# Causal attention in half chunks of 64 tokens, router steps on GpSimd, six sort steps moved behind the attention

## The chip, the cores and the metric

The kernel runs on one core of one Trainium2 chip. The metric is the device time of one execution in microseconds (us). Engines are named as in the profile: PE is TensorE (PEld its weight loads), DVE is VectorE, ACT is ScalarE, POOL is GpSimd, SP is SyncE.

## What is computed

Two transformer blocks on 4 sequences of 1024 tokens with 128 features. The part that changes is the attention of the first block, a causal linear attention with 16 heads of 8 features, each lifted to 64 positive features:

```
q_prime = relu(einsum('bhld,hdm->bhlm', q, proj))
k_prime = relu(einsum('bhld,hdm->bhlm', k, proj))
kv_cumsum = cumsum(einsum('bhlm,bhld->bhlmd', k_prime, v), axis=2)
context = einsum('bhlm,bhlmd->bhld', q_prime, kv_cumsum)
norm = einsum('bhlm,bhlm->bhl', q_prime, cumsum(k_prime, axis=2))
out = context / (norm[..., None] + 1e-06)
```

Behind it stands a mixture of 64 experts, whose router sorts the scores of all tokens for each expert (`order = argsort(-router_scores, axis=0)`, groups of 64 sorted scores, the best groups kept), and then the second block.

## The kernel before

`causal_attention` walks over 32 chunks of P = 128 tokens, 8 chunks to a sequence (`NC`), 4 chunks to a token tile of 512 (`s = t // 4`, phase `ph = t % 4`). Each engine has its program written out by hand, chunk by chunk, and they meet at semaphores. Nothing is scheduled by a tool: an engine does its instructions in the order of its own `chunk(t)`.

What PE does in one chunk: a mask into the bank of the odd heads (L732), the scores of 8 of the 16 heads (`scores(t, 0)`, L739), the chunk's contribution to the running state (`state`, L750), the features of the next chunk (`features`, L705), a transposition of the last chunk's output (`by_token`, L779), the output that comes from the state of the chunks before (`from_state`, L760), the mask and the scores of the other 8 heads (`scores(t, 1)`), `back` (L784), the output that comes from the chunk's own scores in two parts (`from_chunk`, L770), and the keys of the next chunk by token (`keys_by_token`, L716). DVE takes the scores of the even heads out of their bank with the causal mask (L991, twice a chunk), ACT those of the odd heads (L916, twice). DVE adds up the state (L999, L1002) and divides (`divide`, L1009 to L1013). ACT takes out the features (L902) and the keys (L910).

All f32 matmuls are two instructions in the trace. Scores use tiles of the array of 64 rows by 128 columns (even heads in the upper, odd heads in the lower half of the rows), `state` tiles of 128 by 64, `from_state` and `from_chunk` tiles of 128 by 32, `features` and `keys_by_token` of 32 by 128.

Spread over the four phases of a token tile is other work: the projections of the next tile (`project`, L55 to L57, phase 2), `out_proj` (L788), and the router of the last tile: the residual sum (`add_x`, L1020), the layer norm (`centre` L492, `square`, `take_centred` L543, `variance` L497, `normalise` L549 and L551, `h_high`, `h_low` L558), the logits, their softmax and `scores_back`. From chunk 12 on DVE also has steps of the sort in its queue, in four pieces of each chunk (`sort(t, part)`; one step is L449 and L450). `HELD = 25` is the number of steps of the third sort that are done there; the other 20 are done in the next stage, between DVE's router steps for the last tile, before the fourth sort with the experts' `products`.

## Time and profile before

| | us |
|---|---|
| median of 3 runs | 1006.01 |
| lowest, highest | 1004.88, 1008.31 |
| span of the profiled execution | 1005.2 |
| attention, first mask to the end of chunk 31 | 52.3 to 378.7 |
| its tail to the next stage's first instruction | 378.7 to 388.8 |
| mean granted clock of PE over the span | 0.943 |

The span runs from the first to the last instruction and lies 0.8 us under the median; nothing else of the profiled execution's time is known. In the rows, a time is counted from the start of the span. PE works its instructions off in overlap, so the distance from start to start tells what a group costs, not its duration. The granted clock is 1.00 at 2.4 GHz and 0.50 at 1.2 GHz.

### The profile page before, as it was taken

Reading aid. Unit: us, or ns where it says so; the run is one execution under the profiler, and the core shown is the slowest. Engines: PE = TensorE matmul, PEld = TensorE weight load, DVE = VectorE, ACT = ScalarE, POOL = GpSimd, SP = SyncE. Lnnn points to the kernel's source line nnn. Section 1 sums busy time; section 2 is a strip of 40 time slices with the busy share of each in tenths; the row PEclk is TensorE's granted clock in tenths of the full one; section 3 lists DMA queues with packets and bytes.
Section 4 is the critical chain, followed back from the end, with each engine's and each line's share of the span. In section 5 each row is a group of like instructions: output and inputs, shape, how many; then the busy total and the mean of one; then the engine's idle time right before and its main releaser. Section 6 shows DMA issues by size and latency. Waiting matters only on the chain. (4 is left out here: it accounts for less than half of the span.)

```text
span 1005.2 us, 19673 instructions
## 1 busy us (share of the span) xinstructions
PE 862.9 (86%) x7294; PEld 478.1 (48%) x7294; DVE 741.8 (74%) x1404; ACT 456.6 (45%) x810; POOL 181.9 (18%) x150
## 2 busy tenths in 40 slices
PE   7498999999989885799997988999998787699885
PEld 4266666666656551233443432444433555345543
DVE  3535546787878886999978777888887446689985
ACT  4545656566545551566676862111111255423232
POOL 4250000000000001000004584333332000033340
PEclk9779999999989996899998989999999798899998
DMA  4060000000000000366784768787873000000001
GB/s 129 21 146 2 3 3 2 2 3 2 2 3 2 3 1 1 149 259 241 273 303 168 280 237 321 256 280 270 288 262 137 1 1 1 0 11 11 22 11 31
DMA packets 49671, 103.96 MB, mean 103 GB/s; under 512 B 9968, under 2 KB 24112, under 8 KB 49456
## 3 DMA queue, kind: packets, MB, share of 16 engines
q1 hardware_dynamic: 45360, 100.68, 28.4%
q10 hardware_dynamic: 4224, 2.10, 0.8%
q8 instruction: 57, 0.93, 0.4%
q14 instruction: 30, 0.25, 0.1%
HBM read 53.48 MB, written 48.23 MB: 101 GB/s over the span
## 5 line engine op out<-in xcount | busy, mean ns | idle before, releaser
L1231 PE MATMUL bank<-RS,Wd 128*128 128x512 f32 x256 | 131.5, 603 | 8.8 <-DVE RS L1294 8.6
L1294 DVE TENSOR_TENSOR RS<-so_ug,bank 128x512 f32<-128x512 f32 x128 | 84.1, 672 | 24.0 <-PE bank L1217 13.2
L902 ACT ACTIVATE att_qk<-bank 128x512 f32<-128x512 f32 x128 | 66.8, 602 | 45.0 <-PE bank L705 44.6
L1196 POOL TENSOR_TENSOR so_ug<-so_ug 128x512 f32<-128x512 f32 x48 | 62.3, 1298 | 108.6 <-DMA so_ug<-hidden 108.6
L739 PE MATMUL bank<-att_qk 64*128 64x128 f32 x1024 | 77.2, 292 | 0.0
L1231 PEld LDWEIGHTS bank<-RS,Wd 128*128 128x128 f32 x256 | 47.3, 192 | 59.3 <-issue 28.8
L739 PEld LDWEIGHTS bank<-att_qk 64*128 64x128 f32 x1024 | 64.7, 194 | 20.1 <-issue 20.1
L991 DVE TENSOR_TENSOR att_am<-bank,causal 128x512 f32<-128x512 f32 x64 | 44.0, 687 | 40.9 <-PE bank L739 40.9
L1537 POOL TENSOR_TENSOR so_made<-so_ug 128x512 f32<-128x512 f32 x23 | 35.6, 1564 | 155.7 <-DVE bank L1730 144.6
L1560 ACT ACTIVATE so_ug<-bank,bu 128x512 f32<-128x512 f32 x80 | 54.7, 684 | 17.2 <-PE bank L57 17.1
L1510 POOL MEMSET so_below<- 128x128 f16 x1 | 0.2, 205 | 313.1 <-POOLq L142 313.1
L55 PE MATMUL bank<-Hhi,Wgh 128*128 128x512 f16 x128 | 49.7, 388 | 4.9 <-DVE so_made L1688 4.7
L916 ACT ACTIVATE att_am<-bank 128x512 f32<-128x512 f32 x64 | 38.5, 601 | 27.1 <-PE bank L739 26.6
L910 ACT ACTIVATE att_kt<-bank 128x512 f32<-128x512 f32 x64 | 34.7, 594 | 35.0 <-PE bank L716 34.6
L770 PE MATMUL bank<-att_am,att_v 128*32 128x128 f32 x1024 | 41.3, 279 | 10.8 <-DVE att_am L991 9.1
L1898 POOL TENSOR_TENSOR ff_xn_h<-ff_xn_h,la_qT 128x1408 f32<-128x1408 f32 x7 | 22.2, 3172 | 154.3 <-DVE ff_xn_h L99 154.3
L56 PE MATMUL bank<-Hhi,Wul 128*128 128x512 f16 x128 | 50.0, 390 | 0.0
L55 PE MATMUL bank<-Hhi,Wuh 128*128 128x512 f16 x128 | 49.9, 390 | 0.0
L57 PE MATMUL bank<-Hlo,Wuh 128*128 128x512 f16 x128 | 49.8, 389 | 0.0
L56 PE MATMUL bank<-Hhi,Wgl 128*128 128x512 f16 x128 | 49.3, 385 | 0.0
L57 PE MATMUL bank<-Hlo,Wgh 128*128 128x512 f16 x128 | 49.3, 385 | 0.0
L1217 PE MATMUL bank<-F,spread 128*128 (+1 forms) x128 | 48.2, 387 | 1.3 <-ACT F L1456 1.3
(420 smaller groups left out, 1942.2 us busy)
## 6 DMA issues: line engine op xcount, KB each, us to landing
so_ug<-hidden SPq DMA_DIRECT2D x48, 768.0 KB, 5.0
hidden<-so_off SPq DMA_DIRECT2D x48, 512.0 KB, 3.0
hidden<-so_made SPq DMA_DIRECT2D x80, 256.0 KB, 2.1
so_ug<-hidden SPq DMA_DIRECT2D x16, 512.0 KB, 4.2
prep_xin<-in_L_attn_x_dram ACTq DMA_DIRECT2D x8, 256.0 KB, 9.2
out_dram<-ff_ot SPq DMA_DIRECT2D x8, 256.0 KB, 2.3
so_other<-so_key SPq DMA_DIRECT2D x2, 512.0 KB, 5.7
prep_wm<-in_L_wmod_dram SPq DMA_DIRECT2D x2, 384.0 KB, 6.0
```

Source lines behind the costliest of these rows:

```text
L55: nc.tensor.matmul(out, w_hi, x_hi, start=start, stop=False)
L56: nc.tensor.matmul(out, w_lo, x_hi, start=False, stop=False)
L57: return nc.tensor.matmul(out, w_hi, x_lo, start=False, stop=stop)
L739: m = nc.tensor.matmul(psX[half][:, i * P:(i + 1) * P], qk[t % 2][rows, r, 2 + i % 2, :], qk[t % 2][rows, r, i % 2, :], start=half == 0, s ...
L770: m = nc.tensor.matmul(psO[32 * r:32 * r + 32, g * P:(g + 1) * P], v_of(t, 8 * g + 2 * r + half), am[:, g, half, r * P:(r + 1) * P], start ...
L902: nc.scalar.activation(qk[t % 2][:, r, :, :].rearrange("p a l -> p (a l)"), psF[r], ACT.Relu).then_inc(s_["fe"], 1)
L991: nc.vector.tensor_tensor(heads(am[:, g, 0, :]), heads(psX[0]), causal[:].unsqueeze(1).to_broadcast([P, 4, P]), ALU.mult).then_inc(s_["me" ...
L1196: nc.gpsimd.tensor_tensor(u, u, g, ALU.mult).then_inc(s_pp, 1)
L1217: nc.tensor.matmul(psW[k % 4][:, :], spread[:, k, :], F2[:, cols], start=True, stop=True).then_inc(s_W[k % 4], 1)
L1231: nc.tensor.matmul(psY[j][:, :], Wd[:, n, :], hh[n % 4][:], start=False, stop=n == EBLK - 1).then_inc(s_dn[n % 4], 1)
L1294: nc.vector.tensor_tensor(hh[i][:], pg[four % 2][:, i if four % 2 else i // 2 * 3 + i % 2, :], psW[k % 4][:, :], ALU.mult).then_inc(s_hh[k ...
L1560: nc.scalar.activation(to_u, psU[m % 3][:, :], ACT.Silu, bias=bu[:, k:k + 1], scale=1.0 / WS).then_inc(s_u, 1)
```

## The change

Each chunk is worked as two halves of 64 tokens (`HT`). Scores are made within a half only: 32 matmuls of 64 by 64 with 64 rows, on four tiles of the array, and all 16 heads fit in the two banks at once, so the mask matmul, DVE's masked copy and ACT's are done once a chunk instead of twice. What the second half owes to the first goes through the state: there are two states a chunk (`Ss[0]`, `Ss[1]`), `state` is 32 matmuls of 64 rows instead of 16 of 128, DVE adds twice, `from_state` is 16 matmuls of 64 columns instead of 8 of 128, and `from_chunk` 32 of 64 instead of 16 of 128. The values `v1` are kept twice with the other half's rows zero, so that a matmul over 128 rows adds nothing of the other half; the memset of `v1` has twice the size.

The residual sum, the second half of the layer norm (`modulate`) and `h_low` go from DVE to POOL for the first 7 token tiles, and the copy of the centred tile from DVE to ACT (`centred`). `out_proj` and all of the router stand about one phase later. The last softmax within the attention (tile 6) is finished behind chunk 31. The sorts begin a chunk later, and `HELD` is 19: six steps of the third sort go to the next stage's loop.

The diff, cut to its core (removed lines of the functions that are printed above are left out):

```diff
-        HELD = 25
+        HELD = 19
...
                 SORTS = {}
-                for a, counts in enumerate(([6, 6, 6, 6, 6, 5, 5, 5], [8, 8, 8, 7, 7, 7], [7, 6, 6, 6])):
+                for a, counts in enumerate(([6, 6, 6, 6, 6, 5, 5, 5], [8, 8, 8, 7, 7, 7], [7, 6, 6])):
                     first = 0
                     for i, n in enumerate(counts):
-                        SORTS[12 + 8 * a + i] = (a, first, n)
+                        SORTS[13 + 8 * a + i] = (a, first, n)
                         first += n
                     assert first == (len(SORT_LOCAL) if a < 2 else HELD)
-                MERGES = {26: (0, 5), 27: (5, 5)}
+                MERGES = {27: (0, 5), 28: (5, 5)}
...
                         step = Chain(pool, s_["preset"], first=FIRST)
                         step(nc.gpsimd.memset(v1[:], 0.0))
-                        step(nc.gpsimd.memset(v1[:, :, :, :, HD:HD + 1], 1.0))
+                        for j in range(2):
+                            step(nc.gpsimd.memset(v1[HT * j:HT * j + HT, :, j, :, :, HD:HD + 1], 1.0))
...
+                        def residual(s):
+                            cols = slice(s * ST, (s + 1) * ST)
+                            pool.wait_ge(s_["yd"], FIRST + s + 1)
+                            nc.gpsimd.tensor_tensor(XT[:, cols], XT[:, cols], yt[:], ALU.add).then_inc(s_["xu"], 1)
+                        for s in range(NU - 1):
+                            residual(s)
+                            rt.modulate(pool, s, s, ops=nc.gpsimd)
+                            rt.h_low(pool, s, s, ops=nc.gpsimd)
...
+                        def scores(t):
+                            pe.wait_ge(s_["fe"], FIRST + 4 * t + 4)
+                            pe.wait_ge(s_["me"], FIRST + t)
+                            for p in range(NH // 2):
+                                for j in range(2):
+                                    own = slice(HT * j, HT * j + HT)
+                                    for half in range(2):
+                                        rows = slice(64 * half, 64 * half + 64)
+                                        m = nc.tensor.matmul(psX[half][own, p * HT:(p + 1) * HT],
+                                                             qk[t % 2][rows, p // 2, 2 + p % 2, own],
+                                                             qk[t % 2][rows, p // 2, p % 2, own], start=half == 0, stop=True,
+                                                             skip_group_check=True, tile_position=(64 * half, HT * j))
+                                        if p == NH // 2 - 1 and j == 1:
+                                            m.then_inc(s_["Ao" if half else "Ae"], 1)
                         def state(t):
                             pe.wait_ge(*keys_out(t + 1))
...
+                            pe.wait_ge(s_["vd"], FIRST + 2 * (t // 4) + 2)
+                            for p in range(NH // 2):
+                                for j in range(2 if t % NC < NC - 1 else 1):
+                                    rows = slice(HT * j, HT * j + HT)
+                                    for half in range(2):
+                                        h = 2 * p + half
+                                        m = nc.tensor.matmul(added[j][64 * half:64 * half + 64, p * 32:(p + 1) * 32],
+                                                             kt[t % 2][rows, h * MF:(h + 1) * MF], v_of(t, j, h)[rows],
+                                                             start=True, stop=True, skip_group_check=True,
+                                                             tile_position=(HT * j, 64 * half))
+                                    if p == NH // 2 - 1:
+                                        m.then_inc(s_[f"S{j}"], 1)
...
+                            pe.wait_ge(s_["Sv0"], FIRST + t + 1)
...
+                                for j in range(first, 2):
+                                    for r in range(4):
+                                        p = 4 * g + r
+                                        nc.tensor.matmul(psO[32 * r:32 * r + 32, g * P + j * HT:g * P + j * HT + HT],
+                                                         Ss[j][t % 2][:, p * 32:(p + 1) * 32],
+                                                         qk[t % 2][:, p // 2, p % 2, j * HT:j * HT + HT],
+                                                         start=g == 0 and j == first, stop=False, skip_group_check=True,
+                                                         tile_position=(0, 32 * r))
+                        def from_chunk(t):
+                            pe.wait_ge(s_["me"], FIRST + t + 1)
+                            pe.wait_ge(s_["mo"], FIRST + t + 1)
+                            for g in range(2):
+                                for half in range(2):
+                                    for j in range(2):
+                                        for r in range(4):
+                                            m = nc.tensor.matmul(
+                                                psO[32 * r:32 * r + 32, g * P + j * HT:g * P + j * HT + HT],
+                                                v_of(t, j, 8 * g + 2 * r + half), am[:, half, 4 * g + r, :],
+                                                start=False, stop=half == 1, skip_group_check=True,
+                                                tile_position=(0, 32 * r))
+                            m.then_inc(s_["O"], 1)
...
+                        def chunk(t):
+                            s, ph = t // 4, t % 4
+                            if t > 0:
+                                even_bank_taken(t - 1)
+                            scores(t)
+                            pe.wait_ge(s_["Od"], FIRST + t)
+                            if t > 1:
+                                pe.wait_ge(s_["cd"], FIRST + t - 1)
+                            state(t)
                             if t + 1 < NCH:
                                 features(t + 1)
                             if t > 0:
...
+                                pe.wait_ge(s_["Sv0"], FIRST + t + 1)
                                 by_token(t - 1)
...
+                            if ph in (1, 2) and s > 0:
+                                pe.wait_ge(s_["me"], FIRST + t + 1)
+                            pe.wait_ge(s_["mo"], FIRST + t + 1)
+                            if ph == 0:
+                                weights(t)
+                            if ph == 1 and s > 0:
+                                out_proj(s - 1)
+                            if ph == 2 and s > 0:
...
+                                project(s + 1, ph - 1, psX[1])
+                            if ph == 3 and s + 1 < NU:
+                                project_values(s + 1, psX[1])
+                            from_state(t)
...
+                        def masked(t):
                             act.wait_ge(*chunks_out(t))
...
+                            act.wait_ge(s_["Ao"], FIRST + t + 1)
+                            nc.scalar.activation(am[:, 1].rearrange("p a l -> p (a l)"), psX[1],
+                                                 ACT.Relu).then_inc(s_["mo"], 1)
...
+                        def masked(t):
+                            heads = psX[0].rearrange("p (a l) -> p a l", l=HT)
                             dve.wait_ge(*chunks_out(t))
...
+                            dve.wait_ge(s_["Ae"], FIRST + t + 1)
+                            nc.vector.tensor_tensor(am[:, 0], heads,
+                                                    causal[:].unsqueeze(1).to_broadcast([P, NH // 2, HT]),
                                                     ALU.mult).then_inc(s_["me"], 1)
...
+                        def state(t, j):
+                            before = Ss[j][t % 2]
+                            behind = Ss[1][t % 2] if j == 0 else Ss[0][(t + 1) % 2]
                             dve.wait_ge(*chunks_out(t))
...
+                            if j == 0:
+                                dve.wait_ge(s_["S0"], FIRST + t + 1)
+                                dve.wait_ge(s_["Sv1"], states(t))
                             else:
...
+                                dve.wait_ge(s_["S1"], states(t) + 1)
+                                dve.wait_ge(s_["Sv0"], FIRST + t + 1)
+                            if j == 0 and t % NC == 0:
+                                ins = nc.vector.tensor_copy(behind[:], added[j])
+                            else:
+                                ins = nc.vector.tensor_tensor(behind[:], before[:], added[j], ALU.add)
+                            ins.then_inc(s_[f"Sv{j}"], 1)
...
+                            if ph == 3 and s > 0:
+                                rt.normalise(dve, s - 1)
+                            state(t, 0)
+                            if c < NC - 1:
+                                state(t, 1)
                             sort(t, 0)
...
                             if t > 0:
                                 divide(t - 1)
...
                             dve.wait_ge(s_pc, FIRST + N_MASKS)
                             nc.vector.tensor_scalar(bits[:, r, :], kk[:], float(1 << shift), None, ALU.mult)
-                        for i in range(len(SORT_LOCAL)):
-                            sort_local(dve, last, s_sort, FIRST, pads, (rt.done(0, "td"),), i, i + 1)
-                            products((i + 1) * AT_LOCAL // len(SORT_LOCAL) - made_n)
+                        held = len(SORT_LOCAL) - n
+                        local = held + len(SORT_LOCAL)
+                        for i in range(local):
+                            if i < held:
+                                rest(n + i, n + i + 1)
+                            else:
+                                k = i - held
+                                sort_local(dve, last, s_sort, FIRST, pads, (rt.done(0, "td"),), k, k + 1)
+                            products((i + 1) * AT_LOCAL // local - made_n)
                         dve.wait_ge(s_sort, FIRST + len(SORT_LOCAL))
```

The order on PE over one whole chunk of phase 3, before. `att_am` are the masked scores, `att_Ss` the state:

```order
L732 MATMUL bank<-above,identb 128x512
L739 MATMUL bank<-att_qk 128x128 x8
L750 MATMUL bank<-att_v,att_kt 64x32 x16
L705 MATMUL bank<-att_q,projbd 128x128 x8
L705 MATMUL bank<-att_k,projbd 128x128 x8
L779 MATMUL bank<-ident,att_ob 128x128 x2
L760 MATMUL bank<-att_qk,att_Ss 32x128 x8
L732 MATMUL bank<-above,identb 128x512
L739 MATMUL bank<-att_qk 128x128 x8
L784 MATMUL bank<-ident,att_ck 128x128
L770 MATMUL bank<-att_am,att_v 32x128 x16
L716 MATMUL bank<-projbd,att_k 128x256 x4
```

And one chunk now (chunk 4, in which L843 and L844 transpose weights beside it):

```order
L773 MATMUL bank<-att_qk 64x64 x32
L788 MATMUL bank<-att_v,att_kt 64x32 x32
L736 MATMUL bank<-att_q,projbd 128x128 x8
L736 MATMUL bank<-att_k,projbd 128x128 x8
L826 MATMUL bank<-ident,att_ob 128x128 x2
L843 MATMUL bank<-ident,att_w_f 128x128 x3
L844 MATMUL bank<-ident,att_wo_f 128x128
L803 MATMUL bank<-att_qk,att_Ss 32x64 x16
L816 MATMUL bank<-att_am,att_v 32x64 x32
L831 MATMUL bank<-ident,att_ck 128x128
L760 MATMUL bank<-above,identb 128x512
L747 MATMUL bank<-projbd,att_k 128x256 x4
```

The scores are one group of 32 and stand next to `state`; one mask is gone, the other stands behind `back`, ahead of the keys.

The order on DVE in the first part of a chunk of phase 1 with sort steps (`att_sorting`), before:

```order
L1020 TENSOR_TENSOR XT<-XT,att_yt 128x512
L449 TENSOR_TENSOR att_sorting<-att_sorting 128x32x8
L450 TENSOR_TENSOR att_sorting<-att_sorting 128x32x8
L991 TENSOR_TENSOR att_am<-bank,causal 128x512
L1002 TENSOR_TENSOR att_Ss<-att_Ss,bank 128x256
L449 TENSOR_TENSOR att_sorting<-att_sorting 128x64x4
L450 TENSOR_TENSOR att_sorting<-att_sorting 128x64x4
L449 TENSOR_TENSOR att_sorting<-att_sorting 128x128x2
L450 TENSOR_TENSOR att_sorting<-att_sorting 128x128x2
L1009 TENSOR_SCALAR att_den<-bank 128x16
L1011 RECIPROCAL att_rd<-att_den 128x16
L1013 TENSOR_TENSOR att_ck<-bank,att_rd 128x128
```

And a chunk of phase 1 now:

```order
L1060 TENSOR_TENSOR att_am<-bank,causal 128x512
L1078 TENSOR_TENSOR att_Ss<-att_Ss,bank 128x256 x2
L453 TENSOR_TENSOR att_sorting<-att_sorting 128x32x8
L454 TENSOR_TENSOR att_sorting<-att_sorting 128x32x8
L1085 TENSOR_SCALAR att_den<-bank 128x16
L1087 RECIPROCAL att_rd<-att_den 128x16
L1089 TENSOR_TENSOR att_ck<-bank,att_rd 128x128
L453 TENSOR_TENSOR att_sorting<-att_sorting 128x64x4
L454 TENSOR_TENSOR att_sorting<-att_sorting 128x64x4
```

The residual sum is gone from DVE's queue, the masked copy stands first, and the two state sums stand together behind it.

## Rows read from the trace of the kernel before

**Rows 1.** Windows: stretch, length, busy (count) of PE, PEld, DVE, ACT, POOL; clock, DMA.

```profile
93.42:132.34 38.92, 36.86 (x639) 25.36 (x635) 20.93 (x41) 23.71 (x48) 0.00 (x0) 1.00 0.01 3
52.30:180.96 128.66, 121.97 (x2088) 86.18 (x2084) 68.84 (x145) 72.97 (x148) 12.85 (x7) 0.97 0.13 29
180.96:378.70 197.74, 178.33 (x2985) 122.01 (x2984) 161.00 (x412) 110.38 (x224) 0.00 (x0) 0.97 0.01 2
378.70:388.80 10.10, 3.65 (x7) 1.07 (x6) 2.21 (x7) 1.39 (x3) 0.00 (x0) 0.50 0.00 1
388.80:490.00 101.20, 85.62 (x364) 34.48 (x365) 99.13 (x214) 56.47 (x85) 4.95 (x22) 0.92 0.50 193
```

**Rows 2.** Timeline of PE: chunk 3, start and duration in us.

```profile
85.33 0.39 PE L732 MATMUL bank<-above,identb 128*128 128x512 bf16 x1
85.65 1.16 PE L739 MATMUL bank<-att_qk 64*128 64x128 f32 x16
86.74 1.12 PE L750 MATMUL bank<-att_v,att_kt 128*64 128x32 f32 x32
87.80 0.73 PE L705 MATMUL bank<-att_q,projbd 32*128 32x128 f32 x16
...
88.90 0.44 PE L779 MATMUL bank<-ident,att_ob 128*128 128x128 f32 x2
89.27 0.64 PE L760 MATMUL bank<-att_qk,att_Ss 128*32 128x128 f32 x16
89.85 0.39 PE L732 MATMUL bank<-above,identb 128*128 128x512 bf16 x1
90.17 1.16 PE L739 MATMUL bank<-att_qk 64*128 64x128 f32 x16
91.26 0.33 PE L784 MATMUL bank<-ident,att_ck 128*128 128x128 f32 x1
91.52 1.33 PE L770 MATMUL bank<-att_am,att_v 128*32 128x128 f32 x32
92.78 0.71 PE L716 MATMUL bank<-projbd,att_k 32*128 32x256 f32 x8
```

**Rows 3.** Windows of L750, then of L770: matmuls in flight (x) in a stretch.

```profile
213.36:213.42 0.06, 0.05 (x2) 0.05 (x2) 1.00 0.00 0
213.44:213.49 0.05, 0.05 (x4) 0.05 (x6) 1.00 0.00 0
...
218.47:218.55 0.08, 0.08 (x4) 0.08 (x8) 1.00 0.00 0
218.60:218.67 0.07, 0.07 (x8) 0.07 (x5) 1.00 0.00 0
```

**Rows 4.** Groups by line within the attention: busy us, mean ns, idle before and releaser.

```profile
L991 DVE TENSOR_TENSOR att_am<-bank,causal 128x512 f32<-128x512 f32 x64 | 44.0, 687 | 40.9 <-PE bank L739 40.9
L770 PEld LDWEIGHTS bank<-att_am,att_v 128*32 128x32 f32 x1024 | 24.6, 109 | 22.6 <-DVE att_am L991 18.7
L1002 DVE TENSOR_TENSOR att_Ss<-att_Ss,bank 128x256 f32<-128x256 f32 x24 | 10.0, 417 | 4.2 <-PE bank L750 4.2
```

**Rows 5.** Timeline: ACT takes out the keys behind chunk 3's L716.

```profile
93.59 0.60 ACT L910 ACTIVATE att_kt<-bank 128x512 f32<-128x512 f32 x1 [1.37 <-PE bank L716]
```

**Rows 6.** Timeline of DVE: sort steps at the next stage's beginning.

```profile
388.87 0.43 DVE L449 TENSOR_TENSOR so_pad<-keys 128x256 f32<-128x256 f32 x1 [3.64 <-PEq L142]
...
389.66 0.43 DVE L449 TENSOR_TENSOR so_pad<-so_pad 128x256 f32<-128x256 f32 x1
```

**Rows 7.** Sources L1196 (POOL) and L1055 (DVE): duration ns min/median/max.

```profile
L1196 POOL TENSOR_TENSOR so_ug<-so_ug x48: 1261/1272/2298, 599.4 to 769.0; 128x512 f32<-128x512 f32 x48
L1055 DVE TENSOR_SCALAR sgn<-mod x2: 172/2065/3958, 71.4 to 76.0; 128x8 f32<-128x8 f32 x2
```

**Rows 8.** Windows, columns as in Rows 1: the granted clock within chunks 23 and 24.

```profile
288.00:292.00 4.00, 1.75 (x33) 1.17 (x29) 3.86 (x13) 1.50 (x4) 0.00 (x0) 1.00 0.02 4
294.00:302.00 8.00, 8.00 (x94) 5.99 (x86) 3.41 (x10) 2.94 (x7) 0.00 (x0) 0.50 0.01 2
```

401 lines of the change are left out of this document (176 added, 225 removed).

## The prediction

> **What bounds the kernel now.** The chain that ended last covers only the last per cent of the span, so I read the stretches instead, then the chunk. In the windows by stage the attention takes 326.4 us of the 1005.2: 128.66 for chunks 0 to 12 and 197.74 for chunks 13 to 31, with PE at 95% and 90% busy, DVE at 54% and 81%, ACT at 57% and 56% [rows 1]. So PE sets the pace of the early chunks. With the sorts in its queue DVE comes close behind, and the chunks grow from 9.73 us (38.92 over chunks 4 to 7) to 10.41 us on average. Behind the attention DVE is 98% busy for 101 us [rows 1]: what is put into its queue there comes at full price.
>
> The timeline of chunk 3, which has no router or projection in it, shows what a chunk costs PE from start to start [rows 2]: mask 0.32, scores 1.09, state 1.06, features 1.10, transposition 0.37, from_state 0.58, mask 0.32, scores 1.09, back 0.26, from_chunk 1.26, keys 0.64; sum 8.09. The other 1.64 of the 9.73 are the phases' extras.
>
> **The halves on PE.** The windows at single rounds show how the array is fed [rows 3]. L750 (tiles 128 by 64, two side by side): two matmuls in flight, then four about 0.06 us later, so a round of two every 0.058 (32 instructions in 0.93, plus 0.13 for the change of tile shape, is its 1.06). L770 (128 by 32, four side by side): four in flight, then eight 0.11 later; 16 instructions are four rounds, 0.44, and 0.14 for the change makes the 0.58 that L760 has in rows 2. L739 (two tiles, 128 wide): eight rounds of 0.11 are 0.89 of its 1.09. The members of a round start almost together: a round costs its longer side, the weights' columns or the moving columns, 0.11 for 128 and 0.058 for 64, not the number of its instructions.
>
> By that the new groups are, with four tiles in each round: scores 64 instructions, 16 rounds, 0.93 and 0.10 at the start (state has the same shape, no change between): 1.03. State 64 instructions, 16 rounds (64 columns of weights): 1.06. From_state 32 instructions, 8 rounds of 64 columns: 0.46, no change behind it. From_chunk 16 rounds and a change: 1.07. Unchanged: features 1.10, transposition 0.37, back 0.26, one mask 0.32, keys 0.64. Sum 6.31 against 8.09. What goes is one mask (0.32), one round of scores (1.15), and 0.24 of L770's 1.26 in which PE waited for the second masked copy (of such waits L770's weight loads had 18.7 us in all) [rows 4].
>
> One wait is late next. State needs the keys that ACT takes out; the eviction begins 0.81 behind the keys' first matmul [rows 2, 5], and two of 0.60 that overlap a little end at 1.9. PE is at state 0.64 + 1.03 = 1.67 behind it: 0.25 of waiting. ACT's copy of the output stands ahead of that, but its matmuls end a microsecond before. Net gain 1.78 - 0.25 = 1.53 a chunk, and a chunk of 8.2 us with extras.
>
> No row shows 64 by 64 tiles. Bounds: all four at once, as above, or two at a time, which adds 0.93 to scores and to state and gives the gain back. I take the first: rows of one half and columns of one half each ran in parallel in rows 3 and in L739.
>
> Here a rule of the notes speaks against the change. In rows 3 several matmuls share a round of 0.058 or 0.11. The Trainium skill (TensorEngine Tiling, Performance Considerations, Instruction Overhead) says that each matmul has some 60 cycles of overhead and that a dimension that is already small should not be tiled further. At 2.4 GHz an estimate from that page is 25 ns for each of 224 instructions, 5.6 us in place of 3.25, and a total near 1021.
>
> **Early chunks, 0 to 12.** 13 times 1.53, less about 1 because chunk 2 waits for DVE's weight work: -19.
>
> **Late chunks, 13 to 31.** PE: 19 times 8.2 = 156. DVE: it has 161.0 now [rows 1]. Off go 19 masked copies of 0.69 (13.1) and, for 5 token tiles, the residual, the centred copy, the modulation and h_low at up to 0.69 (13.1 together); on come 19 more state sums of 0.42 [rows 4] (8.0) and 4 halves of the values' eviction (2.7). The sort steps between chunk 13 and 31 are as many as before (109 and the merge). That is 145.5, 7.7 a chunk, under PE's 8.2 on average, but a chunk with 7 or 8 steps of 0.79 [rows 6] or a merge needs 9 to 9.7, which makes 8 chunks some 1.2 longer: 165. Before, PE's need was 19 times 9.5 = 180 and the stretch took 197.7, 10% more, for waits of one queue on another. I add 5% to 165, since the unevenness is already counted: 174, so -24.
>
> **POOL in place of DVE.** 21 instructions; POOL's nearest row is 1.27 us for 512 columns [rows 7], so residual, modulate and h_low take 3.8 us of a tile of 33 us, and h_low is wanted by the logits with about half a microsecond to spare. The other price is DVE's: an operation on 8 columns took 3.96 us in chunk 1, against 0.17 for its twin, while POOL worked on weights (12.85 us in that stretch) [rows 1, 7]. Bounds 0, and 15 instructions of 1.27 in the late chunks, 19. Most of DVE's waiting falls into slack: +4.
>
> That row shows it as a stall. The Trainium skill (GPSIMD Engine Reference, Key points) says that GpSimd shares its SBUF interfaces with VectorE and contends with instructions that have two SBUF inputs; every sort step has two, so by the page alone the upper bound would be the estimate, 15 us more than mine.
>
> The doubled memset of v1 ends some 4 us later than now, but the first use of the values is behind the first scores on PE, which run at 1.2 GHz there: nothing, at worst 2.
>
> **Clock.** The granted clock fell to 0.50 for about 10 us after a stretch in which PE was 44% busy, DVE 97% [rows 8]; that chunk cost 12.2. With DVE ahead of PE in 8 chunks I expect one or two such falls more, 3 us each at most: +3, bounds 0 and 10.
>
> **Tail.** It is 10.1 us [rows 1]. Now the softmax of tile 6 is finished there: from its logits at the end of chunk 31 come the maximum, three sort steps, the division and only then the last output's division on DVE, at 0.42 for 256 columns and 0.79 a step; against now I get +3.4 (1 to 6). **The six steps** moved: 6 times 0.79 on a queue that is 98% busy [rows 1, 6]: +4.8, with no cover.
>
> **Sum.** -19 - 24 + 4 + 3 + 3.4 + 4.8 = -27.8 on 1005.2, 977.4. The median lies 0.8 above the span: 978.
>
> **Rivals.**
> (a) *Each small matmul costs what the larger did.* If the instructions, not the rounds, are the price (27.5 ns in L770's rounds), the four groups cost 224 times 0.0275 + 0.37 = 6.5 instead of 3.6, a chunk 9.2 + 1.64 = 10.9, against 9.73 and 10.41: +15 and +11, with 4.8 and 3 behind it 1039. (By the page's estimate above: 1021.) For it: no round in the rows is shorter than 0.058 with two, and nothing shows that PE's queue can be filled with four in 0.058. Against it: four start together in L770. It decides from about 20 ns for each instruction on, where the saved mask and scores are used up: slower than before.
> (b) *64 by 64 tiles run two at a time.* A chunk is 8.2 + 1.64 = 9.8, early +1, late about +2, and the moved steps, tail and POOL +9: 1018. Against it: neither direction is serial in the rows.
> (c) *The gain is eaten by DVE and by waits.* PE's need falls, but the late chunks keep 10% of waits, POOL stalls the sorts by 10, and the clock falls three times: -17 - 12 + 10 + 7 + 8 = -4 to -8, about 1000. For it: DVE was at 81% and will be at 84%.
>
> **How the numbers follow.** Forecast 0.66, (a) 0.14, (b) 0.08, (c) 0.12. The forecast's own range is 955 to 997: early gain 13 to 25, late 12 to 35, and the bounds of POOL, clock and tail. The range, with (c) and (b) in it, is 953 to 1018; (a) and a little below are left out. A measurement can tell 0.3%, 3 us. Faster by more than that: forecast and half of (c), 0.72; within 0.06; slower 0.22.
>
> **What would show it.** In the changed kernel's timeline: scores and state 64 instructions each in 1.0 to 1.1 us (1.9 for rival (b), 1.8 with from_chunk alike for (a)); bare chunks of 6.6; chunks 4 to 7 in 33 us; chunks 13 to 31 in 174 with DVE at 84%; sort steps during POOL's work no longer than 0.42 to 0.8; and a tail of 13.5. Wrong I would be with rounds longer than 0.07, with DVE over 90% busy in the late stretch, or with the clock at 0.50 for more than 30 us of it.

## The result, and the profile after

| | before | after |
|---|---|---|
| median (4 runs each) | 1005.48 us | 976.83 us |
| lowest, highest | 1004.88, 1008.31 | 972.43, 978.75 |
| ratio, 95% interval | | 0.971 [0.968, 0.974] |
| span of the profiled execution | 1005.2 | 970.6 |

The change takes 28.7 us off the median (26 to 32 by the interval). The profiled execution was the shortest of its four, so its span fell by 34.6; a second profile of the same kernel, `again` below, has 977.6. All executions count in the ratios and intervals except the profiled one of held25 (979.25), which is over 1.5% above the fastest of that kernel and so counts as slow. The windows by stage of the changed kernel (stretch, length, busy time and count of PE, PEld, DVE, ACT, POOL; clock, DMA) answer to [rows 1]: chunks 4 to 7, chunks 0 to 12, chunks 13 to 31, and the tail.

```profile
88.00:123.58 35.58, 31.64 (x1080) 24.05 (x1080) 17.81 (x37) 21.56 (x44) 3.21 (x3) 1.00 0.02 5
51.30:165.86 114.56, 98.85 (x3529) 75.95 (x3522) 57.27 (x127) 66.00 (x136) 20.94 (x17) 1.00 0.17 37
165.86:337.00 171.14, 149.99 (x5098) 114.28 (x5095) 153.82 (x385) 101.85 (x209) 17.11 (x15) 0.96 0.02 4
337.00:351.05 14.05, 3.81 (x16) 1.29 (x12) 6.98 (x20) 1.71 (x4) 0.01 (x1) 0.60 0.00 0
```

The early chunks fell by 14.1, the late ones by 26.6; the tail grew by 4.0. The attention begins 1.0 earlier, and from the next stage's start to the end it is 619.6 instead of 616.4, 3.2 more. That is the whole -34.6.

The timeline of PE in chunk 8 (start, duration, what was idle before) answers to [rows 2].

```profile
123.58 1.16 PE L773 MATMUL bank<-att_qk 64*64 64x64 f32 x64
125.11 1.14 PE L788 MATMUL bank<-att_v,att_kt 64*64 64x32 f32 x64 [0.36 <-ACT att_kt L974]
126.17 0.73 PE L736 MATMUL bank<-att_q,projbd 32*128 32x128 f32 x16
...
127.28 0.44 PE L826 MATMUL bank<-ident,att_ob 128*128 128x128 f32 x2
127.55 0.47 PE L849 MATMUL bank<-ident,RS 128*128 128x128 f32 x3
127.95 0.42 PE L803 MATMUL bank<-att_qk,att_Ss 128*32 128x64 f32 x13
128.83 0.30 PE L803 MATMUL bank<-att_qk,att_Ss 128*32 128x64 f32 x3 [0.47 <-issue]
128.96 1.10 PE L816 MATMUL bank<-att_am,att_v 128*32 128x64 f32 x64
129.99 0.33 PE L831 MATMUL bank<-ident,att_ck 128*128 128x128 f32 x1
130.16 0.38 PE L513 MATMUL bank<-ident,att_rt_pr 128*128 128x128 f32 x2
130.37 0.38 PE L760 MATMUL bank<-above,identb 128*128 128x512 bf16 x1
130.68 0.71 PE L747 MATMUL bank<-projbd,att_k 32*128 32x256 f32 x8
131.33 0.39 PE L773 MATMUL bank<-att_qk 64*64 64x64 f32 x10
```

State takes 1.06 from start to start, `from_chunk` 1.03, and scores 1.17 once the 0.36 of waiting for the keys is taken out of 1.53. New is the 0.47 **in the middle** of `from_state`: 13 matmuls, a hole, three more, and nothing is waited for that the profile knows ("issue"). In before no idle time of PE's matmuls within the attention is put down to "issue"; that of its weight loads stood at the beginning of a group, 0.9 at most.

The waits within the attention of after (us in total, times, longest):

```profile
PEld bank L803 <- issue: 13.8, 26, 2.1
PE bank L803 <- issue: 4.2, 3, 2.0
PE bank L788 <- ACT att_kt L974: 6.8, 19, 0.7
```

The page's lines on PE and on the instruction queue (packets, MB, share), of after:

```profile
PE 808.2 (83%) x10846; PEld 458.1 (47%) x10846; DVE 733.8 (76%) x1384; ACT 441.3 (45%) x785; POOL 209.3 (22%) x174
...
q8 instruction: 85, 1.39, 0.6%
```

and of before:

```profile
PE 862.9 (86%) x7294; PEld 478.1 (48%) x7294; DVE 741.8 (74%) x1404; ACT 456.6 (45%) x810; POOL 181.9 (18%) x150
...
q8 instruction: 57, 0.93, 0.4%
```

Matmuls and weight loads together are 21692 for 85 packets and 14588 for 57: **one packet of 16 KB for every 255 to 256 instructions of PE**, in both kernels. So I take a packet to be the next piece of PE's program; three more kernels below keep the ratio. The Trainium skill (Vector Engine (DVE) Microarchitecture Reference, Instruction fetch and dispatch) gives an instruction's width as 64 bytes, told of VectorE; 16 KB are 256 of those, and the counts here agree.

### The profile page after: what moved, and what is told of

Its sections match the earlier page's. It is cut to its first block and busy times, and to the rows that moved or that the text cites. A ratio compares the mean times of both kernels' runs of the same rounds, so it can differ in the third digit from the quotient of the medians.

```text
span 970.6 us, 26710 instructions
## 1 busy us (share of the span) xinstructions
PE 808.2 (83%) x10846; PEld 458.1 (47%) x10846; DVE 733.8 (76%) x1384; ACT 441.3 (45%) x785; POOL 209.3 (22%) x174
## 5 line engine op out<-in xcount | busy, mean ns | idle before, releaser
L1605 POOL TENSOR_TENSOR so_made<-so_ug 128x512 f32<-128x512 f32 x23 | 35.6, 1565 | 160.1 <-DVE bank L1808 150.3
L1060 DVE TENSOR_TENSOR att_am<-bank,causal 128x512 f32<-128x512 f32 x32 | 22.0, 688 | 38.3 <-PE bank L773 38.3
L454 DVE TENSOR_TENSOR att_sorting<-att_sorting 128x256 f32<-128x256 f32 x103 | 49.9, 485 | 0.0
L773 PE MATMUL bank<-att_qk 64*64 64x64 f32 x2048 | 40.5, 229 | 10.2 <-DVE att_rt_pr L582 4.3
L788 PE MATMUL bank<-att_v,att_kt 64*64 64x32 f32 x1920 | 39.7, 226 | 9.2 <-ACT att_kt L974 6.8
L974 ACT ACTIVATE att_kt<-bank 128x512 f32<-128x512 f32 x64 | 34.7, 594 | 26.6 <-PE bank L747 26.6
L453 DVE TENSOR_TENSOR att_sorting<-att_sorting 128x256 f32<-128x256 f32 x103 | 44.7, 434 | 2.3
L773 PEld LDWEIGHTS bank<-att_qk 64*64 64x64 f32 x2048 | 35.4, 142 | 22.2 <-issue 8.0
```

What stands on the lines that cost most here:

```text
L453: nc.vector.tensor_tensor(o[:, :, 0:m], first, second, ALU.max)
L454: return nc.vector.tensor_tensor(o[:, :, m:size], first, second, ALU.min)
L773: m = nc.tensor.matmul(psX[half][own, p * HT:(p + 1) * HT], qk[t % 2][rows, p // 2, 2 + p % 2, own], qk[t % 2][rows, p // 2, p % 2, own], ...
```

## Experiments

All times are medians, and the kernel before ran on the same chip beside each group: 1004.69 beside state3, feat3, serial and held25, 1005.09 beside again, wide, router_dve and pool_more, 1007.03 beside router_late, gates_first and split, 1003.72 beside keys_early.

### PE ahead of its own instructions

In the trace of after, 24 holes of over 0.1 us in PE's work within the attention begin behind the start of such a packet and end 1.1 to 1.5 us behind its landing, about 16.5 us together, of which some 12.5 lie in chunks 0 to 12; before has none such. In five of the 24, some 3 us, the profile names a semaphore that PE waited for, so these may be ordinary waits that met a packet by chance. The stricter count is PE's idle time that is put down to "issue": 14.2 us, 12.0 of them in chunks 0 to 12, and none in before. The largest is in chunk 2, where the packet is under way from 72.74 to 73.82:

```profile
72.81 0.31 PE L803 MATMUL bank<-att_qk,att_Ss 128*32 128x64 f32 x7
75.11 0.38 PE L803 MATMUL bank<-att_qk,att_Ss 128*32 128x64 f32 x13 [1.99 <-issue]
```

Two theories stand against each other: by the rounds theory only the rounds on the array cost time, by the fetch theory PE also waits for the packets of its program. Two kernels add the same array time with more and with fewer instructions. **state3**:

```diff
-                            for p in range(NH // 2):
+                            for k, p in enumerate([*range(NH // 2)] * 3):
...
-                                    if p == NH // 2 - 1:
+                                    if k == 3 * NH // 2 - 1:
```

> The changed kernel with the 32 matmuls of `state` written three times in a row in every chunk (same result, 256 TensorE instructions more a chunk, weight loads counted). Rounds theory (the forecast's): a group costs 16 rounds of 0.058 us, 0.93, so +1.86 a chunk, +58 in all, less what the late chunks hide: 1025 to 1036 us. Instruction fetch theory (new, from the trace of the changed kernel: in the stalls of PE inside a group, a packet of 16 KB of the instruction queue is under way, one for about every 256 PE instructions, and PE goes on 1.2 to 1.5 us behind its landing, 2.2 to 2.8 behind its start): scores and three state groups are 512 instructions that the array could take in 4.0 us, but two fetches last 4.6 to 5.6, so another 0.6 to 1.6 a chunk: 1045 to 1085 us, with stalls inside most of the groups of `state`.

**feat3**:

```diff
-                            for i in range(4):
+                            for n, i in enumerate([*range(4)] * 3):
...
-                                    if i == 3:
+                                    if n == 11:
```

> The counterpart of the run with three `state` groups: the 16 matmuls of `features` three times in a row (32 rows by 128 columns, 8 rounds of 0.11 to 0.116 us a group, so +1.8 to +1.86 a chunk, as much array time as there, but 128 TensorE instructions more instead of 256). Rounds theory: the same time as that run, 1025 to 1036. Fetch theory: about +1.85 a chunk and no new stalls, 1025 to 1036, that is 15 to 50 us less than that run.

Measured: state3 1085.94 (ratio 1.080 [1.075, 1.085]), feat3 1026.76 (1.025 [1.018, 1.031]). Against the 976.83 of after these are +109 and +50: both as the fetch theory has them (state3 at its upper end, 1 us over), and the rounds theory misses state3 by 50. The waits of state3 within the attention:

```profile
PEld bank L788 <- issue: 47.9, 52, 2.7
PE bank L788 <- issue: 35.0, 31, 2.6
```

The packets are 115 for 29372 instructions. PE stands for 35 us inside `state`. Windows of state3 and then of feat3 over chunks 0 to 12 show a second part of the difference, the clock:

```profile
53.82:219.67 165.85, 140.00 (x5125) 113.07 (x5121) 55.48 (x125) 66.36 (x136) 19.79 (x15) 0.88 0.12 27
```

```profile
51.50:190.34 138.84, 127.29 (x4357) 104.28 (x4354) 61.15 (x125) 65.63 (x136) 19.26 (x13) 0.97 0.14 31
```

State3 was granted 0.88 there and 0.93 in the late chunks, feat3 0.97 and 0.99. That is some 60 us more at the half clock (granted 0.50), worth at most 30 of the 59 us between the two. The stalls alone are thus 29 to 59 us, and the traces agree: PE's idle time put down to "issue" within the attention is 46.2 us in state3 and 9.1 in feat3, 37 apart. Whether the stalls brought the clock down was not tried.

**wide** goes the other way: the same array time on fewer instructions.

```diff
-                            for p in range(NH // 2):
+                            for p in range(0, NH // 2, 2):
...
-                                        m = nc.tensor.matmul(psX[half][own, p * HT:(p + 1) * HT],
+                                        m = nc.tensor.matmul(psX[half][own, p * HT:(p + 2) * HT],
```

> The changed kernel with the same array time on fewer instructions: two neighbouring matmuls of scores, of from_state and of from_chunk are one of 128 moving columns instead of two of 64, so that scores have 8 rounds of 0.11 instead of 16 of 0.058, from_state 4 for 8 and from_chunk 8 for 16; 160 of some 542 PE instructions of a chunk (weight loads counted) are gone. It computes other numbers: the first of two heads stands for both, and the first half's state and values for both halves. Rounds theory alone: 16 rounds of 0.11 less 32 of 0.058, the same time within 0.1 a chunk, 973 to 979 us. Fetch theory: PE no longer runs ahead of its instructions, the stalls of 16.5 us nearly go, and early chunks are 9 to 12 us shorter: 959 to 968 us.

**again**, the changed kernel as it is:

> The changed kernel as it is, once more, as the measure for the three runs beside it: 973 to 979 us, with 12 to 20 us of PE standing still behind instruction packets in the attention (16.5 in its first profile).

Measured: wide 961.22 (0.957 [0.952, 0.962]), again 978.97 (0.972 [0.965, 0.979]). PE's idle time put down to "issue" within the attention: 1.3 us in wide, 9.0 in again. Windows over chunks 0 to 12, chunks 13 to 30, and from the next stage to the end, of wide:

```profile
51.20:160.10 108.90, 97.35 (x2518) 72.33 (x2514) 61.57 (x125) 65.81 (x136) 19.25 (x13) 0.97 0.16 37
160.10:324.84 164.74, 141.57 (x3485) 102.65 (x3481) 148.16 (x373) 98.85 (x202) 15.27 (x13) 0.97 0.01 3
345.10:960.60 615.50, 522.35 (x2075) 247.66 (x2075) 493.56 (x813) 245.31 (x396) 152.22 (x117) 0.96 0.43 156
```

and the same stretches of again:

```profile
51.43:170.93 119.50, 103.16 (x3526) 79.87 (x3522) 63.66 (x125) 65.99 (x136) 19.24 (x13) 0.93 0.16 35
170.93:335.11 164.18, 141.83 (x4893) 106.31 (x4889) 147.93 (x373) 98.95 (x202) 15.24 (x13) 0.99 0.02 4
355.43:977.60 622.17, 527.72 (x2075) 251.34 (x2075) 493.33 (x813) 245.65 (x396) 153.75 (x117) 0.94 0.42 154
```

The early chunks are 10.6 shorter than in again and 5.3 shorter than in the first profile of after (114.24 from scores to scores), the late ones the same in all three (164.2 to 164.9). These differences are not the fetch alone. In again PE waited 5.2 us in chunk 2 for VectorE's state sums, in wide 4.0, in the first profile of after not at all (why is told below), and the granted clock of the early chunks was 0.93 in again, 0.97 in wide and 1.00 in after. The time put down to "issue" there, 12.0 in after, 6.9 in again and 1.3 in wide, is the more direct measure: so I estimate that the fetch costs this kernel 5 to 11 us from run to run, nearly all of it in the early chunks. The other 6.7 of the 17 us between the two spans lie behind the attention, where no instruction differs but the clock does (0.96 for 0.94): not the fetch, and with other numbers in the data its cause stays open. So wide met its expectation partly by a gain that the theory does not have.

### Rounds

**serial**: the same score matmuls, one tile of the array after the other.

```diff
-                            for p in range(NH // 2):
+                            for half in range(2):
+                                rows = slice(64 * half, 64 * half + 64)
                                 for j in range(2):
                                     own = slice(HT * j, HT * j + HT)
-                                    for half in range(2):
-                                        rows = slice(64 * half, 64 * half + 64)
+                                    for p in range(NH // 2):
```

> The changed kernel with the same 32 score matmuls in another order: all of one 64 by 64 tile of the array, then the next tile. Rounds theory: now nothing runs beside anything, each of the 64 instructions costs its own 0.058, a group 3.7 us instead of 0.93, +2.8 a chunk, +88 in all: near 1065 us. Rival (a), that an instruction costs its price whatever runs beside it (14.5 ns each here): no change, 974 to 980 us.

Measured 1024.19, a single run, +47. Timeline of PE in chunk 8:

```profile
124.74 3.23 PE L773 MATMUL bank<-att_qk 64*64 64x64 f32 x61
127.76 0.25 PE L788 MATMUL bank<-att_v,att_kt 64*64 64x32 f32 x2
...
128.81 0.73 PE L736 MATMUL bank<-att_q,projbd 32*128 32x128 f32 x16
```

Inside a tile the matmuls start 58 ns apart, one by one; in after four start within 20 ns every 58. Order alone makes 61 of them last 3 us, so rival (a), a price for each instruction whatever runs beside it, is out; that all four tiles take part in after puts out (b), two at a time. The +88 was too much for three reasons to be seen here: at each change of tile three matmuls run beside the next tile's, `state` no longer waits for the keys, and PE's idle time put down to "issue" is down to 0.3 us. From the scores' start to that of the features it is 4.07 against 2.59: 1.48 a chunk, and 32 of them are the 47. A single run can't tell this to a few us.

### What GpSimd's part was worth

**router_dve** takes `residual`, `modulate` and `h_low` back to VectorE.

```diff
-                        for s in range(NU - 1):
-                            residual(s)
-                            rt.modulate(pool, s, s, ops=nc.gpsimd)
-                            rt.h_low(pool, s, s, ops=nc.gpsimd)
...
                             if c < NC - 1:
                                 state(t, 1)
+                            if ph == 1 and s > 0:
+                                cols = slice((s - 1) * ST, s * ST)
+                                dve.wait_ge(s_["yd"], FIRST + s)
+                                nc.vector.tensor_tensor(XT[:, cols], XT[:, cols], yt[:], ALU.add).then_inc(s_["xu"], 1)
+                            if ph == 3 and s > 0:
+                                rt.modulate(dve, s - 1, s - 1)
+                                rt.h_low(dve, s - 1, s - 1)
                             sort(t, 0)
```

> The changed kernel with residual, modulate and h_low back on VectorE (the residual behind the state sums of phase 1, the other two behind those of phase 3; the centred copy stays on ScalarE). The prediction booked 4 us for GpSimd's contention against some 10 of VectorE time saved in the late chunks. By it: VectorE gets 5 times 2.0 = 10 us more in chunks 13 to 31, loses about 7 of stretched sort steps (485 instead of 418 ns on average), and the late stretch grows by 2 to 6, the early one not: 978 to 984 us. Rival, contention costs more than the move saves: 970 to 975.

Measured 1003.05 (0.997 [0.993, 1.000], 10 runs): both expectations missed, and nearly the whole gain of the change is gone. The late chunks (13 to 30) grew from 164.18 to 185.79. DVE's timeline there:

```profile
260.30 0.80 ACT L989 ACTIVATE att_yt<-bank,ga_bo,mod 128x512 f32<-128x512 f32 x1
261.13 0.69 DVE L1167 TENSOR_TENSOR XT<-XT,att_yt 128x512 f32<-128x512 f32 x1 [2.88 <-ACT att_yt L989]
```

and two of DVE's waits (us in total, times, longest):

```profile
DVE XT L1167 <- ACT att_yt L989: 13.4, 5, 3.1
DVE Hlo L574 <- ACT Hhi L536: 7.0, 4, 2.0
```

At the head of its queue DVE stands for ScalarE, 20.4 us in all, with sort steps, `divide` and the next evictions behind it. **router_late** puts the same operations where their input is there, the residual at the chunk's end, the other two behind `values`:

```diff
+                            if ph == 3 and s > 0:
+                                rt.modulate(dve, s - 1, s - 1)
+                                rt.h_low(dve, s - 1, s - 1)
                             sort(t, 1)
...
                             sort(t, 2)
+                            if ph == 1 and s > 0:
+                                cols = slice((s - 1) * ST, s * ST)
```

> Like the run with the router steps back on VectorE (1003 us), but each placed where its input should be there: the residual at the end of the chunk of phase 1, modulate and h_low behind the eviction of the values in phase 3. In that run VectorE stood still for ScalarE at these steps, 13.4 us for `yt` and 7.0 for the high part in chunks 13 to 31, with all its queue behind. Theory, the waits at the head of the queue are the price: they go, what stays is some 10 us of work on VectorE against about 8 of sort steps no longer stretched by GpSimd: 978 to 986 us. Rival, the work itself is the price of VectorE's place there: 993 to 1003.

Measured 980.58, ratio 0.974 [0.971, 0.977]. So the wait was the price, not the work: with the router on VectorE but well placed, the change keeps nearly all its gain, and GpSimd's part is worth 2 to 4 us, about what a measurement can tell. Not all of the difference between the two placements need be the wait itself: the granted clock of chunks 13 to 30 was 0.91 in router_dve and 0.94 in router_late (168.52 us), which is worth at most 7 of the 17 us between these stretches. VectorE was busy for 149.48 us of chunks 13 to 30 in router_late and for 147.93 in again, though some 8 us of work had been taken off it. The next runs show where that went.

**pool_more** adds three idle GpSimd operations behind each `h_low`.

```diff
                             rt.h_low(pool, s, s, ops=nc.gpsimd)
+                            for _ in range(3):
+                                more(nc.gpsimd.tensor_tensor(idle[:], above_f[:], above_f[:], ALU.subtract))
```

> The changed kernel with three more GpSimd operations of 128x512 behind each of the 7 h_low (both inputs and the output are memory of their own, nothing waits for them): about 1.3 us each, 27 us of GpSimd's work more, 20 of it beside sort steps. If a VectorE operation with two inputs is stretched by some 0.4 of the time that GpSimd works beside it (6.7 us of stretch to 17.1 us of work in the late chunks now), VectorE gets 6 to 8 us more, of which half lands on the path: 979 to 984 us. If the stretch only fills waits: 975 to 979.

Measured 987.61 (0.985 [0.981, 0.990]), 9 us over again and over the 979 to 984 expected. Its window of chunks 13 to 30:

```profile
164.03:340.06 176.03, 148.85 (x4893) 113.88 (x4890) 157.96 (x373) 98.50 (x202) 28.75 (x25) 0.92 0.02 4
```

Against again GpSimd works 13.5 us more, DVE is busy 10.0 longer on the same instructions, and the stretch is 11.9 longer: of GpSimd's time three quarters came back as VectorE's. How much of this lies on the path isn't shown: the granted clock was lower too (0.92 for 0.99), some 24 us more at the half clock, which alone could be worth the 11.9.

The mechanism stands in the timeline of again, first at a sort step, then at the gate chain of chunk 1 (128x8):

```profile
215.00 1.50 POOL L705 TENSOR_TENSOR XT<-XT,att_yt 128x512 f32<-128x512 f32 x1 [19.64 <-ACT att_yt L998]
215.30 1.49 DVE L454 TENSOR_TENSOR att_sorting<-att_sorting 128x256 f32<-128x256 f32 x1
```

```profile
65.96 5.37 POOL L697 TENSOR_SCALAR keys<-keys 128x2048 f32<-128x2048 f32 x1
67.42 3.93 DVE L1124 TENSOR_SCALAR mod<-mod 128x8 f32<-128x8 f32 x1
73.39 4.06 POOL L699 TENSOR_TENSOR Wul<-keys,Wuh 128x2048 f16<-128x2048 f32 x1
73.56 3.91 DVE L1130 SCALAR_TENSOR_TENSOR mod<-sgn,mag 128x8 f32<-128x8 f32 x1
```

The sort step should take 0.42; it ends at 216.79, 0.29 behind GpSimd's end at 216.50, as the other four that met a residual did. The small operations (0.17 elsewhere) end at 71.35 and 77.47, with GpSimd's at 71.33 and 77.45. They don't run slower, they **wait until GpSimd's instruction ends**. The state sums, one of whose inputs is in PSUM, met GpSimd 12 times and were never held. Nor was the reciprocal of `divide`, which has one input, in memory (0.25 us at 66.92, while GpSimd worked until 71.33). And once a sort step that began 0.14 us behind GpSimd's instruction, at 191.69, took its 0.42, while that instruction took 1.04 instead of the 0.77 of others of its line: there GpSimd was the one that waited. The Trainium skill (SBUF — State Buffer, SBUF: two separate sides) says just this: an exclusive lock on a shared pair of ports for the whole instruction, not a split of bandwidth; the trace agrees. The 3.96 us of [rows 7] were the same: that operation ended 0.03 behind GpSimd's.

**gates_first** has GpSimd begin its weight work behind that chain.

```diff
+                        pool.wait_ge(s_["gates"], FIRST + 1)
                         for n, (hi, lo), src in (("wr", Wrs, wr_f[:]), ("ew", bd, bd_f[:]), ("ew", Wu, wu_f)):
```

> The changed kernel with one wait more: GpSimd begins its weight work (operations of 5.4, 1.9 and 4.1 us) only when VectorE's chain of small gate operations in chunk 1 is done. In the second profile of the changed kernel three of these, on 8 columns of memory to memory, took 3.9, 1.7 and 3.9 us and ended 0.02 to 0.04 behind the end of a GpSimd operation, and TensorE waited 5.2 for the state behind them; in its first profile the chain ran before GpSimd began and cost nothing. Theory, such an operation of VectorE doesn't share with GpSimd but waits until its instruction ends: no such stretch in chunk 1, 3 to 7 us less than the changed kernel on median: 970 to 975. Rival, the next operations of VectorE between memories (weights of chunks 2 to 4) are caught in its place: 975 to 979, with stretches there.

Measured 974.95 (0.968 [0.965, 0.971]; runs of 970.66 to 975.38, where again had 969.4 to 980.2). No gate operation is held and none of chunks 2 to 4 in its place. The size, 2 to 4 us, is at the edge of what can be told. In again PE waited 5.2 us behind that chain; in the first profile of after the chain ran before GpSimd began, and one later operation was held for 1.6. So part of the spread from run to run of after is whether these two met.

**split** also writes GpSimd's router operations as two pieces of 256 columns; the cut shows the residual, and `modulate` and `h_low` are split alike.

```diff
-                            nc.gpsimd.tensor_tensor(XT[:, cols], XT[:, cols], yt[:], ALU.add).then_inc(s_["xu"], 1)
+                            piece(nc.gpsimd.tensor_tensor(XT[:, a], XT[:, a], yt[:, 0:ST // 2], ALU.add))
+                            nc.gpsimd.tensor_tensor(XT[:, b], XT[:, b], yt[:, ST // 2:ST], ALU.add).then_inc(s_["xu"], 1)
```

> The run before this one with each of the three router operations on GpSimd written as two of 256 columns, the second behind the end of the first. By the theory of waiting for the end of an instruction, a sort step that meets the residual is held 0.3 to 0.5 us instead of the 1.08 of now, and no step takes over 1.0 us; the sum of such stretches in the attention falls from 8.0 to 3 to 5 us: 968 to 974. By sharing (each slows the other in proportion) the sum stays at 7 to 9 us and the time with the run before.

Measured 972.10 (0.966 [0.964, 0.969]), not to be told from gates_first. No step takes over 1.0 us, but the held time of the sort steps is 7.1 us, not 3 to 5:

```profile
208.45 0.96 POOL L722 TENSOR_TENSOR XT<-XT,att_yt 128x256 f32<-128x256 f32 x1 [18.37 <-ACT att_yt L1016]
208.74 0.95 DVE L454 TENSOR_TENSOR att_sorting<-att_sorting 128x256 f32<-128x256 f32 x1
209.49 0.79 POOL L723 TENSOR_TENSOR XT<-XT,att_yt 128x256 f32<-128x256 f32 x1
209.72 0.83 DVE L453 TENSOR_TENSOR att_sorting<-att_sorting 128x256 f32<-128x256 f32 x1
```

Each piece holds a step of its own: the second begins before the next step does and takes the ports first. Splitting shares the hold out, it doesn't remove it. The sum of 7 to 9 us was what sharing predicted, so the sum does not decide between the two readings; the ends of the held steps do, 0.27 to 0.29 behind the end of a piece however late in it the step began.

### The moved sort steps and the wait for the keys

**held25** puts the six steps back.

```diff
-        HELD = 19
+        HELD = 25
...
-                for a, counts in enumerate(([6, 6, 6, 6, 6, 5, 5, 5], [8, 8, 8, 7, 7, 7], [7, 6, 6])):
+                for a, counts in enumerate(([6, 6, 6, 6, 6, 5, 5, 5], [8, 8, 8, 7, 7, 7], [9, 8, 8])):
```

> The changed kernel with the six sort steps put back into the attention (25 steps of the third sort in chunks 29 to 31, 9, 8 and 8 instead of 7, 6 and 6). The prediction charged 4.8 us for them behind the attention, with no cover. If that is so, the next stage is 4.8 shorter; VectorE is 90% busy in the late chunks, so most of it comes back there, +2 to +4: 974 to 976 us. Rival: chunks 29 to 31 are bound by VectorE and take all of it and the tail shifts too: 977 to 979.

Measured 974.01 over all four (0.966 [0.959, 0.974] without the profiled one), but its runs spread from 963.7 to 979.3, so this tells nothing apart. The trace is that of the slowest of them, so it only hints: from the next stage to the end 617.1 us, where after has 619.6 and before 616.4, and chunk 30 is 3.1, chunk 31 with the tail 1.6 longer than in again. In again that last stretch is 622.2. By these numbers the steps cost 2.5 to 5 us behind the attention, and about as much within it; which place is better stays open.

**keys_early** is split with `keys_by_token` ahead of `back` on PE and of `finished` on ACT.

```diff
                             from_chunk(t)
+                            if t + 1 < NCH:
+                                keys_by_token(t + 1)
```

> The run before (gate chain first, GpSimd's router operations in two pieces, 972.1 us) with the keys by token made right behind `from_chunk`, ahead of `back`, the router's matmul and the mask, and on ScalarE taken out ahead of `finished`. It tests the wait that the prediction put at 0.25 us a chunk (0.36 in the traces, 19 times 6.8 us in all: `state` waits for the eviction of the keys). The keys are made 0.5 us earlier; what is late next is `finished`, 0.3 behind the keys. Theory: 0.25 to 0.36 less in most chunks in which TensorE sets the pace, 3 to 7 us: 965 to 969 us, with no wait of `state` for the keys. Rival, in the late chunks VectorE sets the pace and the early ones meet an instruction fetch sooner: 970 to 974.

Measured 971.66 (0.969 [0.966, 0.973]): no gain over split (972.10) that a measurement can tell. The wait of `state` for the keys, 21 times and 7.5 us in split, is gone altogether, and PE's idle time put down to "issue" went from 10.8 to 12.9 us; from the first scores to the last it is 275.5 us against 279.0 in the profiles, of which that of keys_early is the shortest of its six. The median is where the rival put it: what PE no longer waits for here it waits for at least in part elsewhere.

## Why the prediction was right, step by step

The forecast of 978 was right, 1.2 us from the median, and the rounds on which it rests are what the traces show. That the sum came so close is partly luck: its early and late terms were off in opposite directions. In the first profile the terms give -34.6 for the forecast's -27.8. In again, whose span of 977.6 is the forecast's 977.4, the early chunks gained only about 9 us for the expected 19, the late ones 27 for the 17 that are left of 24 with the price of GpSimd and of the clock, and from the next stage to the end it is 5.8 more than before instead of 4.8.

- **Rounds of 64 by 64 tiles: right.** Chunk 8 takes 7.75 from scores to scores. Less the wait of 0.36, the hole of 0.47 and what only this phase has (0.40 of L849, 0.21 of L513) that is 6.31, the sum of the prediction. Serial confirms that the four tiles share the 58 ns.
- **The wait for the keys: right in kind, too small.** 0.36 instead of 0.25 in the chunks that have it. Keys_early shows that it was hardly on the path.
- **Early chunks: -19 expected, -14.1 in the first profile**, and up to 3.9 of these are the clock (1.00 for the 0.97 of [rows 1]). The step that failed is the sum over rounds itself: it took PE's program for free. With 542 instructions in a chunk, weight loads counted, instead of some 320, two packets and more must come in 8 to 9 us, and where scores and `state` stand together PE runs dry. Chunks 4 to 7 took 35.6 instead of 33; their holes without a semaphore are 1.11, 0.74 and 0.42, which are 2.3 of the 2.6. In again PE lost 5.2 us more in chunk 2, behind VectorE's held gate operations.
- **Late chunks: -24 expected, -26.6 measured, and the +4 for GpSimd and +3 for the clock did not come on top.** DVE is busy 153.8 instead of 145.5, 90% and not 84%: the 8.3 more are the 8.0 us in which sort steps were held. So the price of GpSimd was under-sized as VectorE's time (8 for 4), and "5% for waits" over-sized by more: over the 165 without waits, waits, GpSimd and clock together took 6 us, where the prediction had 9, 4 and 3.
- **GpSimd in place of VectorE.** The bounds of 0 and 19 held. That sort steps beside GpSimd would take no longer than 0.8 was wrong: 1.51. I read the 3.96 us of [rows 7] as a stall and priced it by overlap; it was a hold to the end of the other's instruction, and its price is GpSimd's time beside two-input work.
- **Clock: too dear.** The mean granted clock of the late stretch is 0.96 instead of 0.97 [rows 1], which is some 3 us more at the half clock, worth half of that.
- **Tail: 14.05 for 13.5.** Right. **Six steps: 3.2 for 4.8** in the first profile and 5.8 in again; the clock behind the attention differs (0.95 and 0.94), so no more can be told.
- **Rival (c)**, the gain eaten by VectorE and by waits, is half there: GpSimd's hold cost VectorE 8.0 us of the rival's 10, the waits did not come. Router_dve, at 1003, shows what such waits would have taken. What kept them away is where the router's steps stand, more than which engine does them.

## What to carry to other kernels

When a change cuts matmuls into smaller ones that run side by side, count PE's instructions, weight loads too, beside the array's rounds; in these traces PE went on 2.2 to 2.9 us behind the start of a packet for 256 of them, so by my estimate a kernel that does 256 in less has PE wait for its program. An operation given to GpSimd can cost VectorE up to its whole length where VectorE has sort steps or other two-input work in memory beside it: 8.0 us of the 17.1 that GpSimd worked in chunks 13 to 31 of after. What it saves here is above all a wait at the head of VectorE's queue, and moving the operation down the queue to where its input is ready saves nearly the same.

## What the runs showed of the hardware

- PE's program comes in packets of 16 KB, one for every 255 to 257 matmuls and weight loads (57, 65, 85, 101 and 115 packets for 14588, 16700, 21692, 25788 and 29372 in before, wide, after, feat3 and state3). Within the attention a packet took 0.9 to 1.5 us (one 1.7). In 44 of the 45 holes of state3 put down to "issue" PE went on 1.2 to 1.6 behind the landing, 2.2 to 2.9 from the packet's start.
- Four 64 by 64 tiles start one 64-column matmul each within 20 ns, every 58 ns: 14.6 ns a matmul. Alone, one tile starts one every 58 ns. The Trainium skill (TensorEngine Tiling (Array Packing), Instruction Overhead) has some 60 cycles for each matmul, which was 25 ns in the estimate of the prediction; the rows here are below that, and decide.
- VectorE's sort steps (two inputs, 256 columns) and its small gate operations (8 columns, one or two inputs, in memory) that GpSimd held ended 0.27 to 0.29 and 0.02 to 0.03 us behind the end of GpSimd's instruction, whatever their own length. Operations with an input in PSUM and the reciprocal were not held in the same trace.
